# Four output rows of a convolution from six products instead of two rows from four, on one core

## The reference

```
x = x + conv_layer(group_norm(x))
x = x + gated_layer(group_norm(x))
```

## Time and profile before

| | us |
|---|---|
| median of three runs (lowest, highest) | 1928.59 (1928.57, 1929.59) |
| the profiled execution | 1928.66 |
| its span, first to last instruction | 1926.9 |
| TensorE busy in the span | 1869.3 (97%) |
| VectorE busy | 1514.2 (79%) |
| ScalarE busy | 787.3 (41%) |
| GpSimd busy | 487.8 (25%) |

### The profile page before, as it was taken

One profiled execution on the slowest core, in us unless ns is written; L12 is line 12 of the kernel. 1 busy time (PEld: TensorE's weight loads), 2 busy tenths in 40 slices (PEclk: granted clock), 3 DMA queues, 4 the chain that ended last, 5 costly groups with the idle time before them and its releaser, 6 DMA issues.

```text
span 1926.9 us, 24377 instructions
## 1 busy us (share of the span) xinstructions
PE 1869.3 (97%) x8788; PEld 837.4 (43%) x8788; DVE 1514.2 (79%) x2391; ACT 787.3 (41%) x971; POOL 487.8 (25%) x504
## 2 busy tenths in 40 slices
PE   6999999999999999999999999999999999999995
PEld 6544444444444444444444444444444444444442
DVE  5658697886968778797787968779787887968766
ACT  2333434444343443534434343443534434353343
POOL 3102313132222222213132222222213132222212
PEclk9999999999999999999999999999999999999997
DMA  4000010100111010010100111010010100100001
GB/s 165 12 22 23 33 45 23 55 34 28 40 44 35 31 45 34 34 44 22 56 23 33 44 44 35 34 44 34 33 46 22 55 23 34 44 22 22 12 22 55
DMA packets 20541, 72.55 MB, mean 38 GB/s; under 512 B 3072, under 2 KB 3264, under 8 KB 20416
## 3 DMA queue, kind: packets, MB, share of 16 engines
q1 hardware_dynamic: 20416, 70.86, 10.7%
HBM read 37.29 MB, written 33.55 MB: 37 GB/s over the span
## 4 chain that ended last, share of the span: by engine, by line
PE 61%; DVE 28%; issue 6%; ACT 4%; POOL 0%; DMA 0%; DVEq 0%; SPq 0%; ACTq 0%; POOLq 0%
PE pair L388 16%; PE pair L390 16%; PE pair L389 16%; PE L L436 4%; DVE T L265 3%; DVE st L728 3%; DVE lv L759 3%; DVE sb L850 3%; DVE pair L790 2%; PE L L470 2%; PE L L468 2%; DVE pair L789 2%; DVE sa L849 2%; PE pair L366 1%; DVE x L857 1%
## 5 line engine op out<-in xcount | busy, mean ns | idle before, releaser
L388 PE MATMUL pair<-T,WH 128*128 128x504 f16 (+1 forms) x2304 | 875.7, 380 | 8.1 <-DVE T L265 6.4
L389 PE MATMUL pair<-T,WH 128*128 128x504 f16 (+1 forms) x2304 | 874.7, 380 | 2.0 <-issue 2.0
L390 PE MATMUL pair<-T,WL 128*128 128x504 f16 (+1 forms) x2304 | 874.7, 380 | 0.0
L388 PEld LDWEIGHTS pair<-T,WH 128*128 128x128 f16 x2304 | 227.9, 99 | 324.8 <-issue 75.8
L390 PEld LDWEIGHTS pair<-T,WL 128*128 128x128 f16 x2304 | 225.5, 98 | 275.2 <-issue 3.4
L603 ACT ACTIVATE uall<-pair 128x1024 int16<-128x1024 f32 x192 | 195.2, 1017 | 361.5 <-DVE x L815 183.6
L389 PEld LDWEIGHTS pair<-T,WH 128*128 128x128 f16 x2304 | 225.5, 98 | 265.1 <-issue 19.9
L1079 POOL TENSOR_TENSOR fl<-lv,fh 128x1024 f16<-128x1024 f32 x64 | 140.8, 2199 | 735.6 <-DVE fh L768 735.6
L595 ACT COPY m<-pair 128x512 f32<-128x512 f32 x192 | 112.1, 584 | 447.6 <-PE pair L390 447.4
L1071 POOL TENSOR_TENSOR zl<-zf,zh 128x512 f16<-128x512 f32 x120 | 157.7, 1314 | 406.3 <-ACT zh L617 399.2
L833 DVE TENSOR_TENSOR ekv<-L,rec 128x512 f32<-128x512 f32 x61 | 42.2, 692 | 183.9 <-ACT rec L635 183.9
(11 more groups left out here) (133 smaller groups left out, 1798.2 us busy)
## 6 DMA issues: line engine op xcount, KB each, us to landing
xs<-in_x_dram SPq DMA_DIRECT2D x64, 512.0 KB, 4.3
out_dram<-x SPq DMA_DIRECT2D x64, 512.0 KB, 2.8
x<-in_L_conv_g_pos_dram SPq DMA_DIRECT2D x3, 576.0 KB, 10.0
x<-in_L_conv_g_neg_dram SPq DMA_DIRECT2D x3, 576.0 KB, 11.0
x<-in_L_conv_Wm_dram SPq DMA_DIRECT2D x2, 32.0 KB, 10.1
x<-in_L_conv_Wq_dram SPq DMA_DIRECT2D x1, 32.0 KB, 11.1
x<-in_L_conv_Wk_dram SPq DMA_DIRECT2D x1, 32.0 KB, 11.1
x<-in_L_conv_Wv_dram SPq DMA_DIRECT2D x1, 32.0 KB, 10.8
```

Source lines behind the costliest of these rows:

```text
L388: nc.tensor.matmul(to, wh, th, start=fresh and y == 1, stop=False, skip_group_check=True)
L389: nc.tensor.matmul(to, wh, tl, start=False, stop=False, skip_group_check=True)
L390: last = nc.tensor.matmul(to, wl, th, start=False, stop=y == 2, skip_group_check=True)
```

## The change

- **Products.** Four output rows now come from six products of 4 row tiles, 256 columns each (`PRODUCTS = 6`, `QUART` = 256). A step is 6 times 9 = 54 matmuls. Products 2 and 4 fill one half of the pair ("low"), 1 and 3 the other, and 0 and 5 accumulate on the latter.
- **Middle.** `mix_middle` forms plus and minus from the two halves, writes the two inner rows of each four straight to the int16 buffer `u`, and puts the base of the two outer rows back into PSUM: six instructions for two. `adc_round` now reads 512 values, not 1024. `u` is double.
- **Rows.** The rows are combined in fp32 from the unsplit f by VectorE (`transform`, seven instructions, into the single buffer `t32`), then rounded to the high part by ScalarE (`rows_high`, three copies), and the rest is taken by GpSimd (`rows_low`, one instruction over 1536 values). `split_f`'s rounding, `low_part`, and both `winograd_rows` passes go. The next image's `transform` for group 0 stands in step 11.
- **Weights.** The six combinations of the weights are made by VectorE (`weight_sums`) ahead of the transposes on TensorE, which are 6 per weight row in place of 8.
- **Mix.** `gated_high` and `gated_low` go; each mix is two fp32 matmuls over 64 partitions in place of four fp16 ones.
- **Order.** The places of several VectorE and ScalarE steps move, as the last part of the diff shows.

```diff
             def middle(p, parity, n, low, first_image):
...
+                    taps(pair[:, 1, 0:QUART], i, parity, g, 2, True, False)
+                    taps(pair[:, 1, QUART:HALF], i, parity, g, 4, False, True).then_inc(low_ready, 1)
+                else:
+                    taps(pair[:, 0, 0:QUART], i, parity, g, 1, True, False)
+                    taps(pair[:, 0, QUART:HALF], i, parity, g, 3, False, True).then_inc(mid_ready, 1)
...
             def mix(image, k, w):
...
-                pe.wait_ge(o_low, nth(image, NG, k - UNSPLIT if w else k))
-                for h, src in ((0, sa[w]), (1, sbb[w])):
-                    out = banks[w][1 - h]
-                    nc.tensor.matmul(out, wmh[:, :], src, start=True, stop=False)
-                    last = nc.tensor.matmul(out, wml[h][:, :], src, start=False, stop=True)
...
+                    last = nc.tensor.matmul(banks[w][1 - h], wmf[half, :], rec[w][half, :], start=True, stop=True)
...
+            def rows_high(image, parity, g):
+
+                act.wait_ge(t_ready, nth(image, NG, g))
+                for pair in range(3):
+                    last = nc.scalar.copy(T[parity][:, 0, pair, g * TILES:(g + 1) * TILES, :, :], t32[:, pair])
+                last.then_inc(th_ready, 1)
...
                     if cur:
                         copy_m2(p, n, first_image)
...
+                    if cur and n in (0, 2, 5):
...
+                        rows_high(p, parity, (0, 2, 5).index(n) + 1)
...
+                    if nxt and n == STEPS - 1:
+                        rows_high(p + 1, 1 - parity, 0)
...
+            def transform(image, g, p, n):
+
+
+                dve.wait_ge(f_ready, nth(image, NG, min(g + 1, NG - 1)))
+                if not (isinstance(image, int) and image == 0 and g == 0):
+                    dve.wait_ge(th_ready, nth(image, NG, g - 1))
+                    dve.wait_ge(tl_ready, nth(image, NG, g - 1))
...
+                nc.vector.tensor_tensor(flat, f[:, at + 2:at + 2 + ROWS, :], f[:, at:at + ROWS, :], ALU.subtract
+                                        ).then_inc(delta_made, 1)
...
+                nc.vector.scalar_tensor_tensor(out=ab[:, :, :, :].rearrange("p t e w -> p t (e w)"),
+                                               in0=mid[:, :, 0:2 * W], scalar=-4.0, in1=mid[:, :, 2 * W:4 * W],
+                                               op0=ALU.mult, op1=ALU.add).then_inc(ab_made, 1)
...
+                nc.vector.scalar_tensor_tensor(out=t32[:, 0].rearrange("p t e w -> p t (e w)"),
...
+                for e, c in ((0, 2.0), (1, -2.0)):
+                    nc.vector.scalar_tensor_tensor(out=t32[:, 1, :, e, :], in0=delta[:, :, 1], scalar=c,
+                                                   in1=delta[:, :, 2], op0=ALU.mult, op1=ALU.add)
...
+                nc.vector.tensor_tensor(t32[:, 2, :, 0, :], ab[:, :, 1, :], ab[:, :, 0, :], ALU.add)
+                nc.vector.tensor_tensor(t32[:, 2, :, 1, :], ab[:, :, 1, :], ab[:, :, 0, :], ALU.subtract
+                                        ).then_inc(t_ready, 1)
...
             def mix_middle(p, n):
-                pair, m = pairs[n % 3], m2
...
-                nc.vector.tensor_tensor(pair[:, 1, :], pair[:, 0, :], m[:, :], ALU.subtract)
-                nc.vector.tensor_tensor(pair[:, 0, :], pair[:, 0, :], m[:, :], ALU.add).then_inc(mid_mixed, 1)
...
+                nc.vector.tensor_tensor(plus, bank, m2[:, :], ALU.add).then_inc(plus_made, 1)
+                nc.vector.tensor_tensor(minus, bank, m2[:, :], ALU.subtract).then_inc(minus_made, 1)
...
+                nc.vector.scalar_tensor_tensor(out=rows[:, :, 2], in0=tiles(plus, 1), scalar=4.0, in1=tiles(plus, 0),
+                                               op0=ALU.mult, op1=ALU.add)
...
+                nc.vector.tensor_tensor(quarter(bank, 0), quarter(plus, 0), quarter(plus, 1), ALU.add)
+                nc.vector.scalar_tensor_tensor(out=quarter(bank, 1), in0=quarter(minus, 1), scalar=8.0,
...
+                nc.vector.scalar_tensor_tensor(out=rows[:, :, 1], in0=tiles(minus, 1), scalar=2.0, in1=tiles(minus, 0),
...
+                    if cur and n == 0:
+                        transform(p, 1, p, n)
...
+                    if cur and not p_is_first and n == 1:
+                        cubic_f(p, 3)
+                    if cur and n in (2, 5):
+                        transform(p, 2 if n == 2 else 3, p, n)
+                    if nxt and n in (6, 9, 11):
+                        cubic_f(p + 1, (6, 9, 11).index(n))
+                    if nxt and n in (5, 8, 9, 11):
+                        quantise(p + 1, (5, 8, 9, 11).index(n))
...
+                        transform(p + 1, 0, p, n)
...
             def phase(p, parity, images):
                 prev2, prev, cur, nxt = images
                 second = prev and cur
...
                 if cur:
-                    low_part(p, 3)
+                    rows_low(p, parity, 1)
                 if prev:
                     spread_stats(1, p - 1)
                 if nxt:
                     spread_stats(0, p + 1)
                 if prev:
                     scale_z(p - 1)
+                if cur:
+                    rows_low(p, parity, 2)
                 if second:
                     z_low(p - 1, 1 - parity, 0, 0)
                 if nxt:
                     scale_x(p + 1)
                 if second:
                     z_low(p - 1, 1 - parity, 1, 0)
...
+                    rows_low(p, parity, 3)
...
+                    rows_low(p + 1, 1 - parity, 0)
```

More of the change, by code:

```diff
@@ L36 @@
 HALF = PX // 2
-TP = ROWS // 2
+TILES = ROWS // 4
+QUART = TILES * W
 STEPS = NG * NP
@@ L253, in waits_apart, with turn_pair, turned, tap_weights @@
                 eng.wait_ge(s, v)
[L255 to L266, removed]
+        def turn_pair(n):
+            return last_pair if n == 8 else pairs[(n - 5) if n > 5 else n % 3]
+        def turned(n):
+            return turn_pair(n)[:, :, :].rearrange("p a n -> p (a n)")[:, 0:PRODUCTS * P]
+        def tap_weights(i):
+            return gp[:, i * CK:(i + 1) * CK].rearrange("p (c y x) -> p x y c", y=3, x=3)
+        PLACE = ((0, 0), (2, 0), (2, 1), (1, 0), (1, 1), (0, 1))
         block = ctx.enter_context(nc.Block())
+        def f_rows(q):
+            return f[:, 1 + q * ROWS:1 + (q + 1) * ROWS, :].rearrange("p r w -> p (r w)")
         def integers(image, q):
@@ L376, in turn_small, with taps @@
                 nc.tensor.transpose(L[1][:, P:2 * P], wm_in, ident[:, :]).then_inc(small_turned, 1)
-            def taps(out, plane, parity, g, j, fresh):
-                rows = slice(g * TP, (g + 1) * TP)
+            def taps(out, plane, parity, g, j, first, last):
+                pair, e = PLACE[j]
+                tiles = slice(g * TILES, (g + 1) * TILES)
                 out = out.rearrange("p (t w) -> p t w", w=W)
@@ L652, in phase @@
                         z_high(p - 1, 1 - parity, (n - 3) // 2, 0)
-                    if second:
-                        gated_high(p - 1, k, 0) if late else exponent(p - 1, k, 0)
+                    if second and not late:
+                        exponent(p - 1, k, 0)
                     if cur and n % NP == 2:
@@ L889, in phase @@
                         gate(p - 1, k, 0) if late else weighted_values(p - 1, k, 0)
-                    if nxt and n == STEPS - 1:
-                        rows_low(p + 1, 1 - parity, 0)
-                    if second and late:
-                        gated_low(p - 1, k, 0)
-                    if n == STEPS - 1 and cur:
-                        stats_x1(p, parity, 2)
-                    if have and m % NP == NP - 2 and n != 9:
-                        combine_planes(image, m // NP)
-                    if whole:
-                        if n == 7 and second:
-                            second_residual(p - 1, 1 - parity, k, 0)
-                        first_residual(image, mpar, m // NP)
@@ L952, in phase @@
                     gate(p - 1, NG - 1, NG - 1)
-                    for k in range(UNSPLIT, NG):
-                        gated_low(p - 1, k, k)
                     for k in range(NG):
```

411 lines of the change are left out of this document (191 added, 220 removed).

## The result

The changed kernel takes 2207.33 us (median of four executions, 2206.5 to 2208.32) against 1928.91 of the kernel before beside it: a ratio of 1.1444, 95% interval 1.1426 to 1.1462. The forecast was 2128, in a range of 1990 to 2225. Slower was right; 79 us are missing in the sum.

What follows compares the result with a forecast made beforehand. TensorE, busy 97%, was taken to set the pace before; after the change, waits across the engines' queues. Stages 30 + 77 + 19.2 + 4 make a 130 us period; 158 + 14 x 130 + 148 gives 2126, time 2128, range 1990 to 2225.

Steps and rivals of the forecast that it cites:

- Matmuls of 256 columns at 0.11 us: TensorE's steps: 54 matmuls take 5.94 us in place of 7.74, saving 21.6 us an image over 12 steps.
- rival 3: Matmuls of 256 columns take 0.13 us or more: time 2254 at 0.13, 2600 at 0.215; chance 0.05.
- VectorE's prices: 0.33 us a 256-value pass, `mix_middle` 2.5, `transform` 3.7; net +12 us an image, VectorE's list 98 undisturbed.
- Rival 4: scalar_tensor_tensor with two SBUF inputs runs at half rate: 14 us more VectorE work, period 140, time 2268; chance 0.03.
- M(0) to M(3): From the start of `mix_middle(0)` to that of `mix_middle(3)`: VectorE's list bounds it, 30 us against 23.2.
- The boundary: `mix_middle(11)` to the next image's `mix_middle(0)`: TensorE stands 11 us for the rows; 19.2 us against 9.7.
- M(3) to M(11): `mix_middle(3)` to `mix_middle(11)`: 67 us of TensorE work plus waits of 2, 5.8 and 2 make 77, against 82.0.
- The clock: Half rate for some 4 us after stands, at the boundary and after `group_stats`: 4 us lost an image, bounds 0 and 6.
- The queue behind `rows_high(3)`: ScalarE's step 5: the copy waits for `transform(3)`, M(6) is 5 us late, keys of group 1 wait too.
- Ends: Before the second image's `mix_middle(0)` 158 us in place of 149; from the last image's on, 148 in place of 158.
- Rival 1: The lists overlap: the period is VectorE's list with hold-ups, 98 + 8 = 106, time 1792; chance 0.10.
- Rivals 2 and 5: Short waits with the clock up, period 118 to 126, chance 0.20; no change, period 115.5 to 116, chance 0.02.

Runs made afterwards that it cites:

- double_pass: The changed kernel with the first short pass of `mix_middle` (256 values) issued twice, the second into a buffer nobody reads: 2243.47 us.
- less_pe: The changed kernel without the low-weight matmuls of products 0 and 5, 6 of 54 in a step: 2164.53 us.
- early_rows: The changed kernel with the next image's group 0 `transform` in step 10, not 11, and its rounding in ScalarE's step 11: 2060.96 us, ratio 1.0682.
- keep_clock: The changed kernel with 70 unread matmuls of 256 columns ahead of the first matmul of each image but the first: 2204.94 us, ratio 1.1424.
- short_low: The changed kernel with GpSimd's `rows_low` cut from 1536 to 128 values from the third image on, output not the reference's: 2112.81 us.
- low_order: The changed kernel with `z_low` for group 0 and `scale_x` moved ahead of `rows_low(2)` on GpSimd: 2183.58 us, ratio 1.1312.
- three_moves: The changed kernel with the next image's group 0 earlier, `rows_high(3)` behind `copy_m2(6)`, and `z_low(0)` and `scale_x` ahead of `rows_low(2)`: 1997.80 us, ratio 1.0364.

## Why the prediction was right, and where it was short

- **Matmuls of 256 columns at 0.11 us: right.** TensorE's timeline in the tail, each start 0.11 behind the last:

```profile
2130.18 0.27 PE L396 MATMUL pair<-T,WH 128*128 128x252 f16 x1
2130.29 0.27 PE L397 MATMUL pair<-T,WH 128*128 128x252 f16 x1
2130.40 0.27 PE L398 MATMUL pair<-T,WL 128*128 128x252 f16 x1
```

  The loads hide, rival 3 is out, and TensorE's work fell as said. Its busy time fell by 195 us only, not by the 16 x 21.6 = 346 that the forecast took from its work, since it was busy at half rate for 324 us and lost half of them, 162.
- **VectorE's prices: right.** 0.33 a short pass, 3.7 a transform. Rival 4 is out: the two-input form on fp32 took 0.42 us for 256 values, the same as tensor_tensor. (The prediction counted two such passes in a `mix_middle` and five in a transform; the diff has three and four, and the price at half rate would have been 16 us and not 14.)
- **M(0) to M(3): right**, 29.3 for 30, VectorE's list, shown by double_pass and less_pe.
- **The boundary: right**, 21.1 for 21.2 with the clock, shown by early_rows; for the clock's 2 us only single boundaries of keep_clock are a proof.
- **M(3) to M(11): the mis-sized terms.** The forecast had 77 and 2 for the clock; it measured 84.4, and 5.4 x 14 = 76 us is nearly the whole miss of 79 (the ends' 10 more and the first stage's 0.7 an image less cancel). TensorE's timeline, its idle times over 0.1 us and the clock's records added up for each image, splits the 84.4: 67.0 of work as at full rate, what the forecast had; 12.0 of waits, where the forecast had 2 + 5.8 + 2 = 9.8; and 5.4 lost to the clock, half of the 10.9 us that it was busy at half rate, where the forecast had 2. So both the waits and the clock were priced too low.
  - *The waits.* The step said "near step 9 `z_low(3)` holds up VectorE's passes: 2 us". The hold-up was known from the earlier trace rows, but priced as four passes at 3.35 instead of 1.42, as if it were shared out, and put at step 9. `rows_low(2)` stood in the forecast only as a delay of GpSimd's own queue, `rows_low(3)` not at all. In truth they stop VectorE for 2.9 us behind M(3) and 2.2 behind M(6), until GpSimd is through, and the first wait is handed on: 2.9 us of VectorE, then 3.3 in the mean of TensorE at the keys of group 0, for which the forecast had 2. short_low takes 4.1 of the 5.4 away; that run also brings `z_low(0)` forward, and no run parts the two (low_order, which moves the hold-up to another pass, takes 1.3).
  - *The clock.* The forecast counted two dips of 4 us an image, 4 us lost with bounds 0 and 6. TensorE was busy at half rate for 20.3 us an image, 10.1 lost: 2.6 in the first stage, where VectorE sets the pace, 5.4 here and 2.1 at the boundary. In short_low 9.3 us at half rate are left from M(3) to M(11). How much of the 5.4 is on the path isn't shown: in M(4) to M(5) and M(10) to M(11) the dips of every second image count in full, 2.1 us in the mean, but less_pe shows that elsewhere TensorE's time turns into waits, and no run held the clock up in this stretch. What sets off the alternation between images stays open.
- **The queue behind `rows_high(3)`: there, but too dear.** M(6) was 4.27 us late for 5 forecast, and taking it away gave 2.1, since VectorE was late too. As it was one of the waits in the same stage, its error hides the others' in part: that is luck.
- **Ends:** 4 and 6 us more than said. At the start `weight_sums` has one pass (L714) of 3.61 us beside GpSimd's first `rows_low` (36.29 to 39.38), and of 0.84 for the next weight row, where GpSimd is idle: the same hold-up, unpriced.

Rival 1, that the lists overlap, had its test in three_moves: even with the waits reordered the period is 120.4, above 115.7, and VectorE is busy for 94% of it, some 113 us, where the forecast had 98 and 8 of hold-ups. Rivals 2 and 5, periods of 118 to 126 and of 116, are out by the 134.9.

The prediction's closing split, waits of 11, 8 and 8 us and the clock, doesn't add up to its period: with 93 of work it makes 124. By its own stages the waits are 11, 10 and 9.8 and TensorE's work is 95, and these make the 130.

## What to carry to other kernels

Before work is moved from the engine that sets the pace to the one beside it, add up the second engine's whole list with its hold-ups; here 21.6 us an image taken from TensorE's work cost VectorE 17 more of busy time (12 by its passes undisturbed, the rest hold-ups) and made a chain of four engines at each boundary, and the order of the queues decided some 210 us. Price a GpSimd instruction like `rows_low` at its full length on VectorE's list if a pass with two inputs in SBUF can fall beside it, and follow that wait to TensorE. Where waits come in, count the time at half clock stage by stage: here 20 us an image, and not 8. When a change has several parts, time each alone: the mix, the only part that was, made the kernel before 0.5% faster.

## What the runs showed of the hardware

- A VectorE pass with two SBUF inputs waits for the end of the running GpSimd tensor_tensor: 3.31 us for 0.42, and three of 1.37 when GpSimd's 3.1 us are three pieces (3.75 in all). The sum over all short passes hardly changed, 449.4 and 456.0 us.
- The int16 passes at L850 and L853 are held too, 1.67 and 1.68 us beside `z_low` for 0.68 and 1.23; L850 has only one input.
- Seventy unread matmuls held the granted clock at 1.00 over the boundary at 1098 in keep_clock (19.1 us), and the time hardly moved: TensorE was busy at half rate for 20.3 us an image in the changed kernel and for 20.5 in keep_clock, less at the boundary and more between M(3) and M(11).
- Two fp32 matmuls over 64 partitions, in four pieces, pass in 1.06 us to the next matmul's start (1068.82 to 1069.88, clock 1.00 around it), against 0.86 for the four fp16 ones at 0.215.
